# A gated cross-attention block with routed experts on one core: attention's value sums in shorter visits, a sixth score bank in some units, small steps and tiles moved

## What is computed

```python
# x (4,256,128), ctx (4,1601,128); H = 16 heads of 8; E = 8 experts, INTER = 256, top 2
h = layernorm(x)
Q, K, V = h @ W_Q, ctx @ W_K, ctx @ W_V                  # split into 16 heads
attn = softmax(where(mask == 0, -1e9, Q @ K.T / sqrt(8)))
x = x + tanh(g_xattn) * ((attn @ V) @ W_T)
h = layernorm(x)
p = softmax(h @ router_w.T);  w, sel = top_k(p, 2)       # not renormalised
for e in sel: y += w_e * (silu(h @ w1_gate_e) * (h @ w1_up_e)) @ w2_e
x = x + tanh(g_ffn) * y
```

## Time and profile before

| | us |
|---|---|
| three timed runs | 458.17, 463.72, 465.64 |
| median | 463.72 |
| the profiled execution, whole | 459.2 |
| its span on the core, of which the trace tells | 457.0 |
| busy: PE, PEld | 423.8, 234.7 |
| busy: DVE, ACT, POOL | 322.9, 275.2, 114.0 |

### The profile page before, as it was taken

How to read it: one execution, slowest core, us unless ns; L and a number is a source line. 1 busy time by engine, 2 the same in 40 slices (tenths; PEclk the granted TensorE clock), 3 DMA queues, 4 the chain that set the end, 5 groups by cost and what they waited for, 6 DMA issues and landing times.

```text
span 457.0 us, 10129 instructions
## 1 busy us (share of the span) xinstructions
PE 423.8 (93%) x3745; PEld 234.7 (51%) x3747; DVE 322.9 (71%) x704; ACT 275.2 (60%) x578; POOL 114.0 (25%) x254
## 2 busy tenths in 40 slices
PE   7877999999999999999999999999998998888994
PEld 3425455555554544444455444445434666566883
DVE  3981787686768998778799778878986661212787
ACT  4204557676767767767777667767744565565321
POOL 4817633617150132001012300101140000000270
PEclk9999899999999999999999999999967999899998
DMA  7866918186848341331504042331414344535112
GB/s 281 165 158 130 237 68 211 66 193 248 197 157 254 82 92 42 66 68 29 107 2 101 22 94 41 56 88 21 94 30 157 93 111 115 147 94 150 30 52 58
DMA packets 31806, 50.36 MB, mean 110 GB/s; under 512 B 3613, under 2 KB 20189, under 8 KB 31757
## 3 DMA queue, kind: packets, MB, share of 16 engines
q1 hardware_dynamic: 29684, 47.53, 41.2%
q0 software_dynamic: 768, 1.57, 1.2%
q10 hardware_dynamic: 1304, 0.59, 0.5%
HBM read 36.00 MB, written 13.44 MB: 108 GB/s over the span
## 4 chain that ended last, share of the span: by engine, by line
PE 63%; DVE 19%; issue 5%; ACT 5%; DMA 3%; SPq 2%; POOL 1%; DVEq 0%; ACTq 0%; POOLq 0%
PE banks L1414 20%; PE banks L1389 16%; PE banks L1371 12%; DVE chunk_max L978 9%; PE banks L1456 4%; DVE chunk_max L960 3%; ACT probs L836 2%; DMA queries<-neg_rows 2%; PE banks L1265 2%; PE banks L1466 2%; DVE late L1163 2%; PE banks L1478 1%; PE banks L1259 1%; DVE late L1169 1%; PE banks L1310 1%
## 5 line engine op out<-in xcount | busy, mean ns | idle before, releaser
L978 DVE TENSOR_REDUCE chunk_max<-banks 128x1 f32<-128x512 f32 (+1 forms) x390 | 239.4, 663 | 76.2 <-PE banks L1371 74.7
L836 ACT ACTIVATE probs<-banks 128x512 f32<-128x512 f32 x384 | 212.0, 604 | 80.4 <-PE banks L1389 79.2
L1389 PE MATMUL banks<-queries,keys 75*128 75x256 bf16 (+1 forms) x832 | 160.3, 278 | 6.3 <-DVE chunk_max L978 3.5
L1371 PE MATMUL banks<-keys,queries 72*128 72x512 bf16 x480 | 147.1, 339 | 1.7 <-DVE chunk_max L978 1.0
L1389 PEld LDWEIGHTS banks<-queries,keys 75*128 75x128 bf16 (+1 forms) x832 | 68.4, 100 | 85.7 <-DVE chunk_max L978 42.0
L1414 PE MATMUL banks<-probs,value_t 128*9 128x256 f32 x1536 | 97.6, 392 | 0.0
L1414 PEld LDWEIGHTS banks<-probs,value_t 128*9 128x9 f32 x1536 | 37.4, 92 | 47.7 <-issue 9.9
L1371 PEld LDWEIGHTS banks<-keys,queries 72*128 72x128 bf16 x480 | 42.5, 97 | 20.2 <-ACT probs L836 6.6
L1163 DVE SCALAR_TENSOR_TENSOR late<-late,banks 128x256 f32<-128x256 f32 x35 | 14.6, 416 | 38.2 <-ACT late L860 37.6
L610 POOL COPY value_t<-values 128x384 f32<-128x384 f32 x16 | 8.0, 503 | 125.2 <-PE banks L1414 122.1
L860 ACT ACTIVATE late<-banks 128x256 f32<-128x256 f32 x35 | 13.4, 383 | 27.1 <-PE banks L1456 13.9
(11 more groups left out here) (175 smaller groups left out, 358.4 us busy)
## 6 DMA issues: line engine op xcount, KB each, us to landing
keys<-k_parts SPq DMA_DIRECT2D x48, 300.2 KB
keys<-w SPq DMA_DIRECT2D x19, 384.0 KB, 3.2
slot_x<-ctx_in SPq DMA_DIRECT2D x5, 704.0 KB, 4.8
ctx_in<-ctxT SPq DMA_DIRECT2D x3, 800.5 KB, 10.2
k_parts<-split SPq DMA_DIRECT2D x6, 400.2 KB, 9.0
k_parts<-late SPq DMA_DIRECT2D x6, 400.2 KB, 6.7
queries<-q_parts SPq DMA_DIRECT2D x16, 144.0 KB
w<-w SPq DMA_DIRECT2D x1, 2048.0 KB, 13.0
```

The source lines that it names most:

```text
L836: nc.scalar.activation(probs[:, s % (HELD * QH), :], ring[ring_bank["scores", n]][:, :], ACT.Exp, scale=SCALE).then_inc(probs_ready, 1)
L978: nc.vector.reduce_max(dst, src, axis=AX.X).then_inc(chunk_used, 1)
L1371: last = nc.tensor.matmul(dst[:, i * CW[c]:(i + 1) * CW[c]], queries[q][0:ROWS, j, t * P:(t + 1) * P], keys[q][0:ROWS, j, c * BANK:c * BAN ...
L1389: last = nc.tensor.matmul(dst, keys[q][0:KR, j, t * P:t * P + w], queries[q][0:KR, j, :], start=True, stop=not with_mask)
```

## The change

- `visit(u)` is 2 in units 4 to 13 (before: 4, 8, 12).
- The ring gets a sixth bank (bank 6) in the units that hold neither tails nor sparse tiles nor pieces of projections: 5, 6, 7, 9, 10, 11. In unit 15 it has three banks (0, 1, 2).
- One table SPARSE_AT gives turn, up, gate, down and bank of each tile; ups stand two slots behind turns, downs three to seven behind ups. In unit 15 tiles rotate through banks 6, 3 and 4.
- In unit 15 DVE does the copies of rows and results, not ACT.
- `tables` runs one step per slot, slots 5 to 16; `y_places` moves from unit 13 to unit 15; `pick_weights` runs once for three batches in unit 15 instead of once in each of units 5, 9, 13.
- `merge` leaves DVE: ACT scales the gathered rows (`weigh`, behind dense tiles 9, 12, 15), POOL adds them, two adds of 128 x 256 a batch, behind its gathers.

```diff
-RING = 5
+RING, SPARE_BANK = 5, 6
...
-S_TABLE = (5, 5, 6, 6, 7, 7, 8, 8, 10, 10, 11, 11)
-S_Y_PLACES = (13, 14, 15, 16, 17)
-S_SLOT_LOADS, S_ROW_LOADS, S_NEG_LOAD = 12, 16, 18
+S_TABLE = (5, 6, 7, 8, 10, 11, 12, 13, 14, 15, 16)
+S_Y_PLACES = (4, 5, 6, 7, 8)
+S_SLOT_LOADS, S_ROW_LOADS, S_NEG_LOAD = 16, 17, 18
...
+SPARSE_AT = [(FIRST_SPARSE, 20, 22, 23, 26, 6), (FIRST_SPARSE, 24, 26, 27, 30, 6),
...
+LAST_RING, LATE_SCORES = 5, 3
...
-MERGE_AFTER = (12, 14, 15)
+WEIGH_AFTER = (9, 12, 15)
...
+def wide_ring(n):
+
+    b, q = divmod(n // SLOTS, NQ)
+    return 0 < b < B - 1 and q > 0
...
 def ring_tables():
...
+    oldest = [SPARE_BANK] + list(range(RING))
     for n in range(B * NQ * SLOTS):
+        allowed = list(range(RING if n < SLOTS * LATE_UNIT else LATE_SCORES)) + ([SPARE_BANK] if wide_ring(n) else [])
         for kind, m in [("scores", n)] + [("chunk", g) for g in chunks_in(n)]:
-            bank = item % RING
+            bank = [i for i in oldest if i in allowed][0]
+            oldest.remove(bank)
+            oldest.append(bank)
...
 def visit(u):
 
-    return 2 if u % NQ == 0 and u >= NQ else 4
+    return 2 if NQ <= u <= FIRST_SPARSE else 4
...
+            def merge(b):
+
+                steps = Chain(pool, merge_step, b)
+                x1 = x1s[:, b, :, :]
+                for k in range(PICKS):
+                    pool.wait_ge(weighed, PICKS * b + k + 1)
+                    i = COLS * b + k * QT
+                    last = nc.gpsimd.tensor_tensor(x1, x1, y_picked[:, i:i + QT, :], ALU.add)
...
+            def weigh(b):
+                act.wait_ge(picks_ready, 1)
+                act.wait_ge(picked[b], 16 * COLS)
+                for k in range(PICKS):
+                    for t in range(QT):
+                        y = y_picked[:, COLS * b + k * QT + t, :]
+                        last = nc.scalar.activation(y, y, ACT.Copy, scale=pick_w[:, b, t, k:k + 1])
+                    last.then_inc(weighed, 1)
...
+                        for i in sparse_at(TURN_AT, u, s):
+                            if by_dve((u, s)):
+                                rows_copy(i)
...
-                    hold(pe, inner_ready, i if i <= ATTN_UPS else ATTN_UPS)
+                    used = [n for n in range(i) if TILE_BANK[n] == TILE_BANK[i]]
+                    if used:
+                        pe.wait_ge(inner_ready, used[-1] + 1)
```

More of the change, by code:

```diff
@@ L199, with by_dve, copies, wait_copies @@
 STORE_AT = [next_slot(at) for at in COPY_AT]
+def by_dve(at):
+    return at[0] == LATE_UNIT
+def copies(table, n):
+    return sum(not by_dve(at) for at in table[:n]), sum(by_dve(at) for at in table[:n])
+def wait_copies(eng, sems, table, n):
+    for one, count in zip(sems, copies(table, n)):
+        hold(eng, one, count)
 def downs_before(u, s):
@@ L768, in _ @@
             pick()
+            for b in range(SPARSE):
+                merge(b)
         @block.scalar
@@ L1030, in top2 @@
             def top2(b, step):
[L1032 removed]
+                steps = Chain(dve, route_step, 4 * (b - 1) + step)
                 if step == 0:
```

148 lines of the change are left out of this document (82 added, 66 removed).

## The result

| us | before | after |
|---|---|---|
| median of 4 timed runs each | 463.39 (458.17 to 465.64) | 446.52 (444.83 to 448.38) |
| ratio after / before, 95% interval | | 0.967 [0.958, 0.977] |
| profiled execution, its span | 459.2, 457.0 | 447.15, 445.0 |

The ratios and their intervals leave out runs over 1.5% above the fastest of their kernel; medians and ranges hold all.

What follows compares the result with a forecast made beforehand. In attention units neither PE nor DVE alone was the bound: four-tile visits outlast the ring's five banks. Terms -4.2 - 4.2 + 0 + 0.7 - 4.0 - 2.4 = -14.1 took 459.2 to 445.1, plus 2: 447 us, range 439 to 457.

Steps and rivals of the forecast that it cites:

- Plain units: Units 6, 7, 10, 11: visits of two tiles take stalls away, 20.05 to about 19.0 us each, -4.2 together.
- the sum of PE's work, 19.0: Plain unit with PE never waiting: 54 starts 11.9 us, six visits 6.5, the one-tile visit about 0.6.
- after short visits there is hardly a stall left for it: Sixth bank, units 5 to 7 and 9 to 11: 0.3 us more lead, counted inside the 19.0.
- Units 5 and 9: Pick-weight steps leave DVE, with short visits: 19.5 us each, -2.1 each, -4.2 together.
- Some stall stays in the first slots: Units 5 and 9: places and hots precede the maxima there, so 19.5 us instead of 19.0 + 0.2.
- Unit 13: Slower table sends rows late: PE stalls about 7 us, clock fall 2 to 3; about 31.7 us, change 0.
- Rival C: Unit 13: late rows are cheap, clock stays up, chain shorter; -5 there, 440 to 441 us in all; chance 0.15.
- Unit 14: Turns two slots behind an up projection wait 4.3 us for gates, against 3.6 of waits before: +0.7.
- The downs, moved six slots behind, wait no more: Unit 14: down projections, placed six slots behind, were to have no waits left.
- Unit 15: Later downs, row copies by DVE and three tile banks cut PE's waits from about 8.4 to 3.6 us: -4.0.
- The end: Merges leave DVE for ACT scalings and POOL adds, six in 4.3 us: -2.4; -1.4 if POOL contends.
- The 2 us: Whole kernel: added to 445.1 us because the profiled run lay 4.5 below the median, taken for clock falls.

Runs made afterwards that it cites:

- e2: The changed kernel without its sixth ring bank (five banks in units 5 to 7 and 9 to 11); 450.26 us, ratio to before 0.978.
- e1: The kernel before with visits of two tiles in units 4 to 13, five ring banks, all else as before; 449.14 us in one run.
- e5: The changed kernel with 34 matmuls nobody reads placed ahead of unit 13's first turn of rows; 442.73 us in one run.
- e4: The changed kernel with SP issuing each load of rows ahead of its weights in unit 13; 440.20 us, ratio to before 0.957.
- e9: The changed kernel with unit 15's tiles all in bank 6 and its copies back on ACT; 447.73 us in one run.
- e8: The changed kernel with merges back on DVE behind dense tiles 12, 14 and 15, replacing ACT's scalings and POOL's adds; 451.48 us in one run.

## Why the prediction was right, and where it was not

**Plain units (forecast -1.05 each, measured -1.31).** The mechanism held: the busy time of PE hid stalls that long visits cause. Two terms were off. The first is the sum of PE's work, 19.0: it took every chunk at 0.22 us, but the two that hold the 65-column ends take 0.12, and the two transposes share one start (264.07 to 264.30). 50 x 0.22 + 2 x 0.12 + 0.23 + 6 x 1.09 + 0.65 = 18.7, which is the unit. The second is the step "after short visits there is hardly a stall left for it": e2 shows 0.41 us of stalls with five banks. This second error didn't move the sum, which had no stall in it; it gave the short visits the credit for what the bank does.

**Units 5 and 9 (-2.1 each, measured -2.7).** "Some stall stays in the first slots": with six banks it did not, 18.86 is 0.14 over a plain unit, less than the rank matmuls' 0.2. e1 and e2 split it: short visits 1.8 to 2.0, pick weights off DVE 0.3 to 0.4, the sixth bank 0.5.

**Unit 13 (0, measured +1.5).** The hole (7 forecast, 7.30), its cause and the half clock's price (2 to 3, 2.34 by e5) held. What was missed is the second turn, which waits 1.22 us for the gate of the first tile: the working costed a turn two slots behind an up projection in unit 14, and didn't apply it to slot 24 of unit 13, where the same two slots stand. Rival C, the late rows cheap, fell as to the change; e4 shows that its 440 us could be had, by the order of the loads.

**Unit 14 (+0.7, measured +3.0).** The turns' waits came out as forecast, 0.67, 1.22, 1.40 and 1.04 against 0.7, 1.3, 1.2, 1.1. Three things failed. "The downs, moved six slots behind, wait no more": in the change most stand four slots behind their up projection, and one waits 1.08 us, since two downs now stand one slot apart (slots 11 and 12) and the second needs the copy of the first's result. Then the stalls of before: the forecast set 3.6 us of them against the 4.3 of the turns, but in the measure in which the turns make 4.3, the brackets, they are 2.15. (From one start to the next each stall is some 0.16 us longer: about 3.3 us before and 6.1 after.) And the count of steps: unit 13 now takes one up projection and unit 14 seven, where it was six; from start to start its projections take 6.35 us instead of 5.77. By brackets the waits grew by 3.3 us; they are the loss, and the extra projection is about offset by small stalls without a bracket that are gone. No run put the two downs apart and left all else.

**Unit 15 (-4.0, measured -4.6).** The banks are the largest part, as named, and the copies a small one. The forecast had the downs' waits go with the new slots; they are 2.8 us before (0.16, 1.03, 0.82, 0.82) and 2.8 after (0.71, 0.45, 0.82, 0.82), and e9 against e1 shows no gain by the slots. Without the clock fall of before the unit gained 3.0, not 4.6, so that this term came out above its forecast by luck.

**The end (-2.4, measured -2.2).** This came by the means named: e8 gives back the 2.2 us. The forecast of the adds on POOL was the open one: 0.67 us an add if nothing contends, about 1.0 by the ratio in the start-up (whose 1.65 is the mean of one add of 1.15 and two of 1.90). Measured are six in 4.54 us; each takes 0.73 to 0.75, and every second one stands 0.08 behind the one ahead. The Trainium skill's rule that GpSimd shares its SBUF interfaces with VectorE and contends with DVE instructions that have two SBUF inputs ("GPSIMD Engine Reference", Key points) may be at work in the 0.06 us more, but no run here took VectorE away at that place; as a cost it stayed near the lower bound.

**The sum.** The terms gave -14.1 and were -13.1 with the errors above (-5.3 - 5.5 + 1.5 + 3.0 - 4.6 - 2.2); start and unit 0 added 1.0. The attention units brought 2.4 us more and the sparse ones 3.2 less, so errors of opposite sign met. The 2 us were added because the profile before lay 4.5 under its median; after the change the profile (447.15) lies 0.6 above its median (446.52), so that reason didn't hold. They made up for the 2.1 us by which the profile missed the sum's 445.1. That 447.0 came within 0.5 us of the median is in good part luck; the direction and the mechanisms are not.

## What to carry to other kernels

A ring's depth and the length of the longest piece of work between its uses act on the same stall. Look for starts further apart than the shortest distance, not at the busy share, and expect two remedies for one stall to overlap (0.8 and 0.9 alone, 1.3 together). When the producer of a table gets slower, look at what its consumer sends first: one queue that issues the large loads ahead of the small one that is needed first cost 6 us here, and a change of order gave them back. Look at the clock of a unit in both profiles before giving its gain to the change: 1.6 us of unit 15's were a clock fall. And when steps are moved over a unit's border, count them again in each unit, and give two steps with one result buffer their distance.
